# Attention kernel in four layers: projections of the first layer in one-pass parts, and a new order of a DMA queue and of GpSimd's work

## What is computed

```python
def layer0(x, ctx):
    h = ln(x, g1, b1)                       # causal self-attention, stage SELF0
    q, k, v = split(h @ qkv_w.T + qkv_b)
    x = x + attend(q, k, v, causal=True) @ proj_w.T + proj_b
    h = ln(x, g2, b2)                       # cross-attention on ctx, stage CROSS0
    x = x + attend(h @ q_w.T + q_b, ctx @ k_w.T + k_b, ctx @ v_w.T + v_b) @ ca_w.T + ca_b
    h = ln(x, g3, b3)                       # MLP0
    return x + gelu(h @ fc_w.T + fc_b) @ proj2_w.T + proj2_b
# layer 1: cross-attention with weights quantized to -1, 0, 1 (CROSS1)
# layer 2: masked self-attention (SELF2), cross-attention (CROSS2), MLP2
# layer 3: causal self-attention with heads of 64 (SELF3)
```

## Time and profile before

| | |
|---|---|
| median of 3 runs | 3846.8 us (3839.29 to 3864.33) |
| profiled execution, its own time | 3851.18 us |
| its span, first instruction to last | 3849.1 us |
| mean granted TensorE clock | 0.963 of 2.4 GHz |

### The profile page before, as it was taken

One profiled execution on the slowest core, in us unless ns is written; L12 is line 12 of the kernel. 1 busy time (PEld: TensorE's weight loads), 2 busy tenths in 40 slices (PEclk: granted clock), 3 DMA queues, 4 the chain that ended last, 5 costly groups with the idle time before them and its releaser, 6 DMA issues.

```text
span 3849.1 us, 69127 instructions
## 1 busy us (share of the span) xinstructions
PE 3607.1 (94%) x21778; PEld 2053.1 (53%) x21778; DVE 2775.6 (72%) x6841; ACT 2455.8 (64%) x5254; POOL 2132.5 (55%) x2103
## 2 busy tenths in 40 slices
PE   6999999999998999999999999999899999999998
PEld 3444444444884444333333344444787777776776
DVE  4566677776676788789999878776766666666664
ACT  2555567777333777778888877776236666666664
POOL 3465544332344555378988843422436767776765
PEclk8999999999997999989999999998899999999998
DMA  4433344432003534333222243431100000000000
GB/s 109 100 83 81 85 107 86 86 84 50 20 1 67 112 86 95 86 74 76 60 61 67 59 107 85 91 83 41 46 6 6 12 12 7 12 12 7 12 7 6
DMA packets 135374, 220.50 MB, mean 57 GB/s; under 512 B 42721, under 2 KB 44641, under 8 KB 133217
## 3 DMA queue, kind: packets, MB, share of 16 engines
q1 hardware_dynamic: 135008, 216.02, 25.0%
HBM read 59.69 MB, written 5.51 MB: 17 GB/s over the span
## 4 chain that ended last, share of the span: by engine, by line
PE 58%; DVE 16%; POOL 11%; ACT 5%; issue 5%; DMA 3%; SPq 1%; DVEq 0%; POOLq 0%; ACTq 0%
PE MX L703 17%; PE L L703 14%; PE OUT L703 12%; PE ST L703 11%; DVE mx L1523 4%; POOL prob L1968 3%; DVE h_lo L1566 2%; DVE h_hi L1564 2%; POOL prob L2040 2%; ACT prob L1262 2%; DVE MX L1516 1%; PE L L928 1%; PE MX L1069 1%; POOL lo L1958 1%; DMA stk<-mrows 1%
## 5 line engine op out<-in xcount | busy, mean ns | idle before, releaser
L1262 ACT ACTIVATE prob<-ST 128x512 f32<-128x512 f32 (+3 forms) x2304 | 1149.8, 572 | 428.2 <-PE ST L703 423.2
L1523 DVE TENSOR_REDUCE mx<-MX 128x1 f32<-128x512 f32 x1536 | 961.8, 682 | 199.0 <-PE MX L703 198.2
L703 PE MATMUL MX<-stk 48*128 48x512 f32 (+3 forms) x2560 | 913.6, 444 | 92.8 <-DMA stk<-lo 27.8
L703 PE MATMUL ST<-stk 50*128 50x512 f32 (+3 forms) x2560 | 934.4, 446 | 5.6 <-ACT prob L1262 4.2
L703 PEld LDWEIGHTS MX<-stk 48*128 48x128 f32 x2560 | 424.4, 191 | 678.5 <-DVE mx L1523 277.8
L2040 POOL TENSOR_SCALAR prob<-prob,mx 128x128 f32<-128x128 f32 (+3 forms) x512 | 557.2, 1101 | 278.9 <-DVE mx L1714 278.9
L703 PE MATMUL OUT<-prob,V 128*32 128x512 f32 (+3 forms) x5120 | 667.9, 595 | 10.7 <-ACT prob L1272 6.0
L703 PEld LDWEIGHTS ST<-stk 50*128 50x128 f32 x2560 | 428.0, 189 | 56.6 <-ACT prob L1262 23.5
L1516 DVE CUSTOM_DVE_ANT_0 MX<-MX,W_even 128x512 f32<-128x512 f32 x512 | 347.2, 700 | 40.0 <-PE MX L703 39.7
L1968 POOL TENSOR_TENSOR prob<-prob,W_odd 128x512 f32<-128x512 f32 x256 | 324.0, 1282 | 76.0 <-ACT prob L1262 75.5
L1520 DVE CUSTOM_DVE_ANT_0 MX<-MX,later 128x128 f32<-128x128 f32 (+3 forms) x512 | 237.2, 518 | 129.3 <-PE MX L703 128.4
(11 more groups left out here) (238 smaller groups left out, 7527.8 us busy)
## 6 DMA issues: line engine op xcount, KB each, us to landing
stk<-hi SPq DMA_DIRECT2D x640, 128.0 KB, 3.8
stk<-lo SPq DMA_DIRECT2D x320, 128.0 KB, 3.9
misc<-misc SPq DMA_DIRECT2D x160, 128.0 KB, 2.8
sums<-spread SPq DMA_DIRECT2D x80, 256.0 KB
ctx_full<-in_ctx_t SPq DMA_DIRECT2D x24, 512.0 KB, 6.9
W_even<-in_w SPq DMA_DIRECT2D x2, 2048.0 KB, 11.3
XH<-in_ctx_rows SPq DMA_DIRECT2D x8, 512.0 KB, 3.6
X<-in_x_t SPq DMA_DIRECT2D x1, 3584.0 KB, 14.7
```

Source lines behind the costliest of these rows:

```text
L703: return nc.tensor.matmul(o, l, r, start=start, stop=stop)
L1262: nc.scalar.activation(prob_at(k)[:, q0:S], STB[k % RING][:, q0:S], ACT.Copy if addmask else ACT.Exp).then_inc(ex_done, 2 if addmask else 1)
L1523: nc.vector.tensor_reduce(m, bank[:, :], AX.X, ALU.max).then_inc(mx_red, 1)
```

## The change

- In SELF0, K, Q, V and O become three-part products of fp32r operands, as do Q and O in CROSS0. Each fp32 matmul (two records) becomes three fp32r matmuls.
- The parts of the weights: for SELF0 ScalarE copies four pieces and VectorE subtracts four, before the first slot; for CROSS0 GpSimd makes them in slot 14 of SELF0, and copies one piece in slot 14 of CROSS0. The MLP0 weights are loaded in two halves, since their upper half's place holds parts until then.
- The parts of the normalized rows: `normalized` now does two activations out of L in SELF0, CROSS0 and CROSS1, first the fp32r part and then `hT`, and only the second frees L. VectorE subtracts (`low_part`) in the even slots, after the second and the third run. GpSimd no longer does this in CROSS1.
- The parts of the output: VectorE makes them for SELF0 (a copy and a subtraction in each slot, after run 8 in even slots and run 10 in odd ones), GpSimd for CROSS0 as for CROSS1.
- SyncE's queue, in all five attention stages: `max_rows` of the first group stands between `stack` kind 0 and `stack` kind 1.
- GpSimd's order, in all five attention stages: `split` for queries stands ahead of the scaling.

```diff
@@ sync: load_weights, slot
-                n = WCOLS if s in MLP_NO else WCOLS // 2
-                sp.dma_start(W[s % 2][:, 0:n], wts[s]).then_inc(w_in[s], 16)
+                n = WCOLS if s == MLP2 else WCOLS // 2
+                sp.dma_start(W[s % 2][:, 0:n], wts[s][:, 0:n]).then_inc(w_in[s], 16)
...
+                    if (s, u) == (CROSS0, UNITS - 1):
+                        sp.wait_ge(ends_low, 3)
+                        sp.wait_ge(l_full, L_NO[s, u - 1, "O1"] + 1)
+                        sp.dma_start(W[0][:, 2048:4096], wts[MLP0][:, 2048:4096]).then_inc(w_upper, 16)
...
                     if on["a"]:
-                        for kind in range(2):
-                            stack(U + 2, half, 0, kind)
+                        stack(U + 2, half, 0, 0)
+                    if on["m"]:
+                        max_rows(U + 1, 1 - half, 0)
+                    if on["a"]:
+                        stack(U + 2, half, 0, 1)
                     if on["b"]:
                         move_few(U, half, 0)
-                    if on["m"]:
-                        max_rows(U + 1, 1 - half, 0)
@@ tensor: project_out, slot
+                    if so in PARTS_NO:
+                        source, w = produced(so, last_batch), weight_parts(so, 3, last_batch and so == CROSS0)
+                        for n, (x, y) in enumerate(THREE):
+                            for k in range(2):
+                                last = mm(Lt[:, t, :], source[x][:, k, tok], w[y][:, k, :], n == 0 and k == 0, n == 2 and k == 1)
+                        continue
...
+                                    if sa == SELF0:
+                                        pe.wait_ge(h_low, NC * ba + cc + 1)
                                     if sa == CROSS1:
                                         project_signs(1, half, source, cc)
-                                    elif cross_a:
-                                        project_parts(0, half, source, cc)
+                                    elif sa in PARTS_NO or cross_a:
+                                        project_parts(weight_parts(sa, 1), half, source, cc)
@@ scalar: normalized, self_weights
                     act.wait_ge(l_full, job + 1)
+                    if sa in PARTS_NO:
+                        nc.scalar.activation(normed(sa, ba)[0][:, c, :], L[:, :], ACT.Identity, **scale_shift(sa, c)).then_inc(h_high, 1)
                     nc.scalar.activation(hT[:, c, :], L[:, :], ACT.Identity, **scale_shift(sa, c)).then_inc(l_free, 1)
@@ vector: slot
+                        if half == 0 and u >= 0 and on["a"] and sa in PARTS_NO and r in (1, 2):
+                            dve.wait_ge(l_free, L_NO[(*kq_slot(U + 1), "T0") if r == 1 else (s, u, "T1")] + 1)
+                            low_part(sa, a_of(s, u, b)[1], r - 1)
+                        made = s - 1 if u == 0 else s
+                        if on["tail"] and made == SELF0 and r == (10 if half else 8):
+                            output_parts(made, UNITS - 1 if u == 0 else u - 1)
...
+                    dve.wait_ge(raw_scaled, N + 1)
+                    nc.vector.tensor_copy(high, raw[:, v % 2, :]).then_inc(raw_high, 1)
+                    dve.wait_ge(raw_high, N + 1)
+                    nc.vector.tensor_tensor(low, raw[:, v % 2, :], high.bitcast(F32), ALU.subtract).then_inc(at_ready, 1)
@@ gpsimd: slot
-                    if s == CROSS1 and u >= 0 and half == 0 and on["a"] and a_of(s, u, b)[0] == s:
-                        for kind, job in enumerate((L_NO[s, u - 1, "T0"], L_NO[s, u, "T1"])):
-                            pool.wait_ge(l_free, job + 1)
-                            normed_parts(b + 1, kind)
...
+                    if on["a"]:
+                        split(u, U, half, 1)
                     if on["tail"]:
                         for g in range(2):
                             pool.wait_ge(raw_in[g], 16 * U)
                         pool.wait_ge(spread_in, 16 * U)
-                        into_parts = (s - 1 if u == 0 else s) == CROSS1
+                        made = s - 1 if u == 0 else s
+                        into_parts = made in PARTS_NO
                         nc.gpsimd.tensor_tensor(raw[:, 1 - half, :], raw[:, 1 - half, :], sums[:, 1 - half, :],
                                                 ALU.mult).then_inc(raw_scaled if into_parts else at_ready, 1)
-                        if into_parts:
-                            output_parts(UNITS - 1 if u == 0 else u - 1)
-                    if on["a"]:
-                        split(u, U, half, 1)
+                        if into_parts and made != SELF0:
+                            output_parts(made, UNITS - 1 if u == 0 else u - 1)
```

More of the change, by code:

```diff
@@ L275, in program @@
         KV_NO = {CROSS0: 0, CROSS2: 1}
+        PARTS_NO = {SELF0: 0, CROSS0: 1, CROSS1: 2}
+        SELF_ORDER = (1, 0, 2, 3)
         JOINED = (CROSS0, SELF2, CROSS2)
@@ L324, in ctx_no, with normed, produced, weight_parts @@
             return NB * CROSS_NO[s] + b
+        def normed(sa, ba):
+            return hT_hi["layer0" if sa != CROSS1 else "later" if ba else "first"], hT_lo
+        def produced(so, last):
+            return raw_hi["layer0" if so != CROSS1 else "last" if last else "early"], raw_lo
+        def weight_parts(so, m, last=False):
+            if so == SELF0:
+                return self_hi[:, m, :, :], self_lo[:, m, :, :]
+            if m in (1, 2):
+                return kv_hi[:, m - 1, :, :], kv_lo[:, m - 1, :, :]
+            return out_hi[:, :, :] if last else ends_hi[:, m // 3, :, :], signs[:, m, :, :]
         def sign_of(m):
@@ L823, in slot @@
                                 begin(u, f"O{part}")
+                                if (s, u) == (SELF0, 2):
+                                    pe.wait_ge(self_low, 4)
+                                if (s, u) == (CROSS0, 2):
+                                    pe.wait_ge(ends_low, 2)
                                 project_out(se, part, se != s)
@@ L951, in last_out @@
                     pe.wait_ge(l_free, L_NO[s - 1, UNITS, f"O{j}"])
-                    project_out(s - 1, j)
+                    if s == MLP0 and j == 0:
+                        pe.wait_ge(ends_low, 3)
+                    project_out(s - 1, j, True)
                 def batch(b):
@@ L1289, in split_weights @@
                         cut = weight_cut(k)
+                        if s == MLP0 and k == 4:
+                            act.wait_ge(w_upper, 16)
                         nc.scalar.activation(w_part(w_hi, cut), w_part(W[s % 2], cut), ACT.Copy).then_inc(wf_hi_done, 1)
```

111 lines of the change are left out of this document (83 added, 28 removed).

## The result

The changed kernel takes 3918.4 us (median of 4 runs, 3913.4 to 3920.7), against 3853.2 for the kernel before beside it (3839.3 to 3864.3). The ratio is 1.0169, 95% interval 1.0131 to 1.0208: 65 us slower, where the sum had 29 and the range ended at 3900.

The account below looks back on a forecast made before the run. TensorE's queue was taken to set the end in SELF0 and CROSS0. Terms -29.1 + 14.3 + 25.7 + 15.2 + 3 = +29.1 us gave 3876 us, 0.75% slower, counted as within 1%; range 3845 to 3900.

Parts of the forecast that it names:

- Queue of SyncE, +25.7: SELF0, CROSS0, CROSS2: queries' stacks behind rows of maxima stall slot starts; with CROSS1's gain, 25.7 us lost (12 to 40).
- The gain of 5 us in CROSS1: CROSS1 slot starts: with the rows of maxima ahead of the stacks, each starts 0.3 us earlier, 16 times.
- Rivals A and B: A: TensorE's gain comes, stack and O0 losses hidden, 3835 us, chance 0.10; B: stacks land sooner, 3828 us, chance 0.07.
- A second read of L, +14.3: M1 behind T1 in SELF0, CROSS0, CROSS1: waits 0.65 us longer, 22 times, 14.3 us lost (0 to 17.8).
- TensorE's blocks, -29.1: Shorter fp32r blocks save TensorE 19.4 us in SELF0 and 9.7 in CROSS0, together 29.1 us gained.
- Rival C: TensorE's gain is hidden because VectorE and ScalarE pace the tiles: 29.1 us more, 3905 us, chance 0.10.
- GpSimd's order, +15.2 in SELF2: SELF2: O0 starts 1.9 us later in 8 slots because the scaling follows the split for queries; 15.2 us lost.
- The earlier stacks buy nothing: Step in the GpSimd order term: making the queries' split sooner gains no time; only SELF2 pays, 15.2 us.
- VectorE, GpSimd, the weights' parts, +3: Added copies and subtractions on VectorE, moved GpSimd work and making the weights' parts: 3 us lost (0 to 16).
- Rival D: SELF0: VectorE held by the later scaling in even slots, 1.3 us in 16 slots, 21 us: 3897 us, chance 0.18.

Follow-up runs that it names:

- run 8: Not a follow-up run: the point in VectorE's order in SELF0's even slots after which it makes the output's copy and subtraction; no time of its own.
- the opposite experiment: Changed kernel with both old orders, first product done twice in SELF0's and CROSS0's one-pass blocks, 23 us of added matmuls: 3904.5 us, 1.0115.

## Why the prediction was wrong, step by step

The waits came in the sum as forecast; the sum was short by 36 us (+29 for +65; beside the first experiments' runs of before, at 3856.7, the changed kernel is 62 slower, and the shares below are of these). The two profiled executions put the miss in one place. TensorE's idle time grew by 62 us, where the terms for waits and other engines' work had 58 (14.3 + 25.7 + 15.2 + 3). Its busy time should have fallen by 29.1 and rose by 8.

**The step that failed: the sum let nothing depend on TensorE's clock.** I read the clock in the earlier trace rows and left it out, without a reason: each wait was priced at its own length, and each block at its length in the earlier trace rows. But the changed kernel runs at 0.951 for 0.960, and 20 of the 62 us are clock by the 40 runs of the kernel before; in the two profiled executions, at 0.951 and 0.963, the 37 us between the busy time forecast and measured are what was missed. The queue's order alone cost 56 us, where 38 stay at equal clock and TensorE's idle time grew by 31; T1's second read cost 35, where 17 stay at equal clock. Both show it within a stage: the same TensorE instructions in SELF0, nearly the same sum of waits, and the stage 30 and 23 us longer with TensorE "busy".

**Queue of SyncE, +25.7.** The waits were sized well (1.66 and 1.03 us for 1.8 and 0.95), and undoing the order in the changed kernel gives 27 us back, 37 at equal clock. On the kernel before it is 56, or 38 at equal clock. At the ends of even slots of SELF0 I took 0.25; on the kernel before it is 0.2, in the changed kernel 0.8 to 1.1. The gain of 5 us in CROSS1 was not there: the slots start on the stacks after, with about the same wait (16.4 us in 14 slots, for 18.4 in 12). Rivals A and B are out. The landing time of the profile's page, not the smaller one of the fit in the Trainium skill (DMA: Bandwidth & Descriptors, Anatomy of one DMA), was the one to use.

**A second read of L, +14.3.** For T1 the term measured 17 us at equal clock, within its bounds, and 35 with the clock. T0's was taken as free; in M1's wait it isn't (1.47 us for 0.92), and at equal clock it adds 12 us, but in the time as measured nothing. That M1 waits for L to be read was right and was not the cause in full: freeing L sooner took 13 us from M1's waits and gained nothing. That it is ScalarE's own time that has to be paid is my reading and is not shown. In the changed kernel M1's waits grew by 7 us in all (13.0 for 5.9 in the three stages), half of the term.

**TensorE's blocks, -29.1.** The lengths were right, and the opposite experiment got 22 of 23 us. Rival C (the gain is hidden) is out in its own form. But with both reads' 28 to 31 us on the other side the edit as a whole can gain nothing, and undoing it in SELF0 cost nothing.

**GpSimd's order, +15.2 in SELF2.** O0 waits 2.34 us as forecast (16.5 us in 7 slots), SELF2 is 20 longer. "The earlier stacks buy nothing" was read from SELF2 alone and was wrong for CROSS1, where they buy 23 us. That gain needs the old queue: with the rows first they have left the stacks' way already, and the changed kernel got neither. So the rows first spoil what the split first offers.

**VectorE, GpSimd, the weights' parts, +3.** At equal clock the kernel with both old orders is 7 us slower: -29 + 28 for the two reads leaves some 8 here, inside the 0 to 16. Rival D is out: VectorE does wait for the scaling in SELF0, but 5.8 us in 7 slots and 1.0 at most in the changed kernel, where D needed more than 1 in each of 16, and giving the work to GpSimd costs more.

At equal clock the changed kernel is 42 us slower, with neither new order 7, with GpSimd's alone 4, with SyncE's alone 25, and the clock's 20 come on top. So the rows first cost 18, and the split first gains 3 without them and costs 17 beside them. Each of these is the mean of 4 runs and moves with the price of the clock, so a few us either way mean nothing.

What stays open: why the fill restored the clock in one kernel and not in the other, why the mean clock fell to 0.946 when the waits at the slot starts were taken out of the changed kernel, and which of the remaining waits, or the shorter blocks themselves, hold its clock at 0.951. MLP0 took 284 to 294 us in the profiled executions of kernels that don't touch it, so its 9 us in the changed kernel are not put down to the loading in halves.

## What to carry to other kernels

Before pricing a new wait on TensorE, look at the clock of the stage: where it is already under 1, as in SELF0 (0.94), one more wait of 0.8 to 1.7 us in every pair of slots made the stage 23 and 30 us longer, two to four times what the added waits sum to. Where it was 1.00, as in CROSS0, waits of about a microsecond cost their length; with M1 waiting 1.3 to 1.5 us there it fell to 0.96 and 0.97, and the stage was 10 and 17 us longer, though freeing L sooner did not bring that clock back. When a shorter block is bought with more work on another engine, measure that work alone first: here ScalarE's extra read, by itself, cost 31 us, as much as the shorter blocks were to gain (29). And when slots start on a DMA, follow the queue back to what the transfer ahead of it waits for; moving that producer forward in every stage but the one where it delayed other work was worth 30 us, 20 of them in the one stage with such a wait.

## What the runs showed of the hardware

- The same program varied by 0.9% (3835 to 3870 us) with its mean granted clock (0.966 to 0.953), 2.25 us per 0.001 over 40 runs and 1.9 over 27 later ones. Comparing the clocks beside the times tells which differences of some 10 us belong to the program.
- Six useless matmuls in every other slot of SELF0, and four in two other stages, made a kernel 19 us faster, while its mean clock went from 0.9525 to 0.9632. In another kernel the same fill brought SELF0's clock from 0.87 to 0.92 and gained nothing in all.
- TensorE's busy time rises as its clock falls: the same instructions of SELF0 were busy 409.7 us at 0.94 and 436.5 at 0.86, so a stage can get longer with its waits unchanged.
